# Two graph layers on one core: table joins spread, fetched rows joined later, small weights prepared ahead

## What is computed

```python
h = maximum(layernorm(x), 0)
x = x + max over neighbours j of h[j, :]          # layer 0
h = maximum(layernorm(x), 0)
hw = h @ W;  a1, a2 = a[:128, 0], a[128:, 0]
e = (hw @ a1)[:, None] + (hw @ a2)[None, :]
e = where(e > 0, e, 0.2 * e); e = where(adj > 0, e, -9e15)
x = x + elu(softmax(e, axis=1) @ hw)              # layer 1
```

## Time and profile before the change

| | |
|---|---|
| runs | 738.23, 739.4, 741.63 us; median 739.4 |
| profiled execution | 738.5 us, its span (first to last instruction) 736.6 us |
| PE busy | 643.8 us, 87% |
| DVE busy | 564.0 us, 77% |
| POOL busy / ACT busy | 366.4 us, 50% / 306.1 us, 42% |
| mean granted clock of PE | 0.956 |
| moved by DMA | 173.32 MB, 235 GB/s on average |
| take of pair 0 / of pair 127 / first weights of layer 1 start at | 25.85 / 438.87 / 448.88 us |

### The profile page before, as it was taken

The page is one execution under the profiler, slowest core; times in us unless marked ns, Lnnn a source line. Parts: engine busy times, 40 slices in busy tenths (PEclk is TensorE's granted clock), DMA queues, the critical chain, the costliest instruction groups (busy, mean ns, idle before and its releaser), DMA issues.

```text
span 736.6 us, 15876 instructions
## 1 busy us (share of the span) xinstructions
PE 643.8 (87%) x6200; PEld 525.3 (71%) x6200; DVE 564.0 (77%) x1296; ACT 306.1 (42%) x554; POOL 366.4 (50%) x357
## 2 busy tenths in 40 slices
PE   1849999899999999799899567989689999999994
PEld 0536667667777677576577356889588999999994
DVE  9829666767868786677768379789578999889893
ACT  1735556567667665466457325514033111001000
POOL 0512147657677765777767776645200474214030
PEclk9988999999999999999999868999989999999998
DMA  9999999999999997999889941428332445444400
GB/s 298 315 392 339 408 339 338 337 345 336 326 349 342 326 319 230 240 362 385 264 248 204 303 151 40 154 84 203 108 115 63 177 151 183 164 138 151 149 16 17
DMA packets 66925, 173.32 MB, mean 235 GB/s; under 512 B 7984, under 2 KB 12720, under 8 KB 62624
## 3 DMA queue, kind: packets, MB, share of 16 engines
q1 hardware_dynamic: 53776, 138.75, 53.9%
q0 software_dynamic: 13072, 33.51, 16.7%
HBM read 125.37 MB, written 46.86 MB: 234 GB/s over the span
## 4 chain that ended last, share of the span: by engine, by line
PE 52%; DVE 15%; DMA 14%; POOL 11%; issue 7%; ACT 1%; DVEq 0%; SPq 0%; POOLq 0%; ACTq 0%
PE pick_ps L756 20%; PE pick_ps L638 10%; POOL found L409 7%; DMA found<-subset_max,rows_at 5%; PE late_ps L651 5%; PE late_ps L652 5%; PE late_ps L614 5%; PE order_ps L623 5%; DVE weight L1174 4%; DMA edge_units<-edge_t 4%; DVE acc L908 3%; DMA subset_max<-keys 2%; PE late_ps L647 1%; DMA limit<-subset_max,spill_rows 1%; POOL h_lo L349 1%
## 5 line engine op out<-in xcount | busy, mean ns | idle before, releaser
L409 POOL DMA_INDIRECT found<-subset_max,rows_at x256 | 256.6, 1002 | 143.0 <-issue 58.9
L756 PE MATMUL pick_ps<-keys,weight 128*128 128x129 f32 x1792 | 214.5, 281 | 18.3 <-DVE weight L1174 18.3
L756 PEld LDWEIGHTS pick_ps<-keys,weight 128*128 128x128 f32 x1792 | 209.6, 197 | 23.8 <-DVE weight L1174 21.9
L1174 DVE SCALAR_TENSOR_TENSOR weight<-limit,curves_sb,stage 128x512 f32<-128x512 f32 x256 | 199.8, 821 | 14.5 <-PE pick_ps L756 2.0
L908 DVE TENSOR_TENSOR acc<-pick_ps,acc 128x1024 f32<-128x1024 f32 x120 | 146.5, 1221 | 69.3 <-PE pick_ps L638 68.5
L447 ACT ACTIVATE first<-order_ps 128x1024 f16<-128x1024 f32 x128 | 131.0, 1023 | 122.8 <-PE order_ps L623 120.7
L652 PE MATMUL late_ps<-bit_n,first 128*128 128x128 f16 x1024 | 131.5, 222 | 0.0
L651 PE MATMUL late_ps<-bit_w,edge_t 128*128 128x128 f16 x1024 | 131.4, 222 | 0.0
L638 PE MATMUL pick_ps<-first,h_hi 128*128 128x512 f16 x256 | 99.7, 390 | 18.5 <-DVE acc L908 18.4
L614 PEld LDWEIGHTS late_ps<-ident_h,stage 128*128 128x128 f16 x1024 | 69.5, 100 | 60.8 <-ACT edge_t L440 14.6
L652 PEld LDWEIGHTS late_ps<-bit_n,first 128*128 128x128 f16 x1024 | 101.8, 99 | 8.2 <-issue 0.6
(11 more groups left out here) (197 smaller groups left out, 570.2 us busy)
## 6 DMA issues: line engine op xcount, KB each, us to landing
stage<-adj SPq DMA_DIRECT2D x64, 1024.0 KB, 9.4
edge_units<-edge_t SPq DMA_DIRECT2D x64, 512.0 KB
stage<-edge_units SPq DMA_DIRECT2D x32, 1024.0 KB, 4.9
subset_max<-keys POOLq DMA_DIRECT2D x13, 512.0 KB, 8.3
found<-subset_max,rows_at POOLq DMA_INDIRECT x256, 6.7
best<-x SPq DMA_DIRECT2D x4, 512.0 KB, 6.3
subset_max<-x POOLq DMA_DIRECT2D x4, 512.0 KB, 10.6
spill_max<-keys POOLq DMA_DIRECT2D x4, 512.0 KB, 14.0
```

Of the source, the lines that this page charges most:

```text
L409: nc.gpsimd.indirect_dma_start(found[:, n % NG, s, :], None, subset_max, bass.IndirectOffsetOnAxis(rows_at[:, n, s:s + 1], 0)).then_inc(ga ...
L756: last = nc.tensor.matmul(out_ps(q, b), weight[:, n % WEIGHTS, b * P:(b + 1) * P], wh[:, c, :], start=c == 0 and starts(q, b), stop=c == C ...
L1174: V.scalar_tensor_tensor(out=weight[:, n % WEIGHTS, :], in0=limit[:, q % 4, :], scalar=slope[:, c:c + 1], in1=units[:, m % EDGES, k * TI:( ...
```

## The change

- **Tables.** The joins 0 to 3 stay behind takes 0 to 3; the others follow two takes apart, behind takes 6, 8, ... 18 (`CHAIN_AT`). The four clears leave the end of the table stores and stand ahead of the fetches of blocks 4, 6, 8 and 10.
- **Ring.** `KEPT` is 4. The room comes from `weight`, which now lies in `first`; the lists' buffers move to the second half of `keys` (`spare_room`). One small constant is dropped (`tri_h`, for which `order_w` with another offset serves), another is f16 (`places`).
- **Joins of fetched rows.** The first two blocks of a tile are joined at pairs 15, 0 and 1 instead of 13 to 15 (11 to 13 in the last tile), the other two at pairs 8 to 10 instead of 5 to 7 of the next tile. Blocks 24, 25 are joined behind the loop; those at mixes 5, 40, 46, 56 move to 18, 42, 60, 67; the one at 33 stays.
- **Lists.** Fetched ahead of blocks 18, 26 and 30 (before: 16, 24, 31), stored ahead of 20, 28, 31, loaded ahead of 21, 28, 31. Joined at take 101, mix 2 and mix 52 (before: takes 88, 121, mix 50). Merged at take 112 and mixes 20, 58 and 68, the last list in halves (before: take 102, ahead of layer 1, mix 58).
- **Small weights.** `W` and `a` are loaded ahead of x; POOL widens `a` before its first work on `h_lo`; PE transposes `W` ahead of the first `flip` and multiplies behind it; ACT's three copies stand ahead of its first root and behind its third `select`.

```diff
-        KEPT = 3
+        KEPT = 4
-        weight = sb("weight", [P, 6, TI], F32)
+        CHAIN_AT = (0, 1, 2, 3, 6, 8, 10, 12, 14, 16, 18)
+        spare_room = keys[:, 1, :, :].rearrange("p r w -> p (r w)")
+        weight = first.rearrange("p s w -> p (s w)").bitcast(F32).rearrange("p (s t) -> p s t", t=TI)
...
+                sp.dma_start(w_sb[:, 0:D], w).then_inc(w_in, 16)
+                sp.dma_start(a12[:, 0:1], a[0:D, :]).then_inc(w_in, 16)
+                sp.dma_start(a12[:, 1:2], a[D:2 * D, :]).then_inc(w_in, 16)
                 for i in range(4):
                     sp.dma_start(xs[:, i * QUARTER:(i + 1) * QUARTER, :], x_rows[:, i * QUARTER:(i + 1) * QUARTER, :]).then_inc(x_in[i], 16)
                 for n in range(STAGES):
                     load(n)
-                sp.dma_start(w_sb[:, 0:D], w).then_inc(w_in, 16)
-                sp.dma_start(a12[:, 0:1], a[0:D, :]).then_inc(w_in, 16)
-                sp.dma_start(a12[:, 1:2], a[D:2 * D, :]).then_inc(w_in, 16)
...
+                    if n in (4, 6, 8, 10):
+                        i = n // 2 - 2
+                        nc.gpsimd.dma_start(spill_dram[:, i * QUARTER:(i + 1) * QUARTER, :], spare(3)).then_inc(spill_clear, 16)
+                    if n in (18, 26, 30):
+                        spill_fetch((18, 26, 30).index(n))
+                    if n in (20, 28):
+                        spill_store((20, 28).index(n))
+                    if n in (21, 28):
+                        spill_load((21, 28).index(n))
+                    if n == 31:
+                        spill_store(2)
+                        spill_load(2)
...
-                    if g < len(CHAINS):
-                        chain(g)
+                    if g in CHAIN_AT:
+                        chain(CHAIN_AT.index(g))
...
-                    if q >= 1 and p >= 13 and q < LAST:
-                        halve(ROWS * (q - 1), 2, p - 13)
-                    if q >= 2 and 5 <= p < 8:
-                        halve(ROWS * (q - 2) + 2, 2, p - 5)
-                    if q == LAST and 11 <= p < 14:
-                        halve(ROWS * (q - 1), 2, p - 11)
+                    if 2 * STEPS - 1 <= g < PAIRS - 1 and (g + 1) % STEPS < 3:
+                        halve(ROWS * ((g + 1) // STEPS - 2), 2, (g + 1) % STEPS)
+                    if g >= 2 * STEPS + 8 and 8 <= p < 11:
+                        halve(ROWS * (q - 2) + 2, 2, p - 8)
```

117 lines of the change are left out of this document (53 added, 64 removed).

## The result

The changed kernel took 710.7 us (median of 4 runs, 705.3 to 712.3), the kernel before 738.8 in the same comparison: a ratio of 0.960, with a 95% interval of 0.954 to 0.966. The forecast was 709.5, the range 700 to 724. The profiled execution took 712.3 us (span 710.5), against 738.5 (span 736.6).

What follows compares the result with a forecast made beforehand. PE sets the pace at 2.78 us a pair, so only longer steps can be won. Terms -6 - 9.5 + 1 + 2 - 9 - 12.3 + 4.6 = -29.2 us from 738.5 gave 709.5 us, range 700 to 724.

Steps and rivals of the forecast that it cites:

- Table joins: Opening, behind take 4: the fifth join, moved behind take 6, waits 8.8 us instead of 14.33; -6 us (bounds -2, -9).
- Edge ring: Takes 19 and 36 to 40: a fourth slot and spread clears remove both late-store waits; -9.5 us (bounds -5, -9.7).
- Price of the spread: After take 18: POOL's fetches start about 6 us late, join at take 31 just in time; +1 us (0 to +6).
- Start: Before take 0: loads of W and a ahead of x delay everything by 1.0 to 5 us; +2 us.
- Joining later: Takes 88 to 110: first list and blocks 18, 19 joined later, so waits for fetched rows go; -9 us (-6, -10.5).
- End of layer 0: Takes 121 to 125: blocks 24, 25 fetched before the second list, joined behind the loop; -12.3 us (-9, -13.3).
- Layer 1: From first weight to end: moved joins and merges cost time; five parts together +4.6 us (bounds -1 and +11).
- (a): Mix 17: joins of blocks 26, 27 and merge of list 1 where DVE has no weights stored; +2.6 us.
- (b): Third list, from known to merged: 37.3 us unchanged; DVE still waits some 9 us, in one place.
- (c) to (e): Later joins +1.5, block 31 just in time for mix 67 +1, half the merge at mix 58 gone -0.5.
- Bound by bytes: Opening, 25.8 to 93 us: DMA limited near 365 GB/s, less won, POOL's start later; 719 us, chance 0.17.
- Layer 1 at its upper bound: Blocks 30 and 31 queue behind list 3, joins stall: +11 instead of +4.6, 716 us; chance 0.15.

## Why the prediction was right, point by point

- **Bound of the kernel.** Right: PE's pace of 2.78 us a pair is unchanged (takes 24 to 28 need 10.97 us in every kernel here), and the gain came from the longer steps alone.
- **Table joins, -6.** Measured -5.8; a wait of 8.2 us where 8.8 was said, because the store took 15.1 us and not 15.9. Undoing the spread gave 4.6 of it back in these takes, and 2 to 4 us net.
- **Edge ring, -9.5.** Measured -4.4 and -6.5, together -10.9, beyond the bound of -9.7, and half of the cause was wrong. The wait at take 19 went because the clears no longer stood in one burst: it is gone without the fourth slot, and in the kernel before with the clears alone moved. The prediction names slot and clears and books both waits to the ring as one term; that the first came out at -4.4 says nothing for the ring. The second is the slot's with 4.1 of 6.5 us. In return the ring is needed near take 100 as well (3.7 us), which the prediction doesn't have.
- **Price of the spread, +1.** Measured +1.0 for takes 19 to 36. POOL's first fetch came at 101.1 us, near the 100 that was said, but 15.2 us behind take 18 and not 12.5. So the join behind take 31, forecast as just in time, waited 3.6 us; 2.2 were caught up by take 36. The number is right partly by luck, as the wait was not in it.
- **Start, +2.** Measured +1.5, by the loads of x. The copies on ACT cost nothing, as said; with x first they did, because `a` then landed later, the exception that the prediction had made.
- **Joining later, -9.** Measured -9.0; the old places of the list cost 6.3 us of waiting and 6 us in all.
- **End of layer 0, -12.3.** Measured -12.6. The place of the join carries 8 to 9 us of it; the order of the fetches, which the prediction also named, hardly matters. The rest, with the early attention vector, was not undone by itself.
- **Layer 1, +4.6: the term that was mis-sized.** Measured +8.4 from one execution to the other. Its parts: (a) mixes 0 to 28, forecast +2.6, measured 47.9 - 43.5 = +4.4; (b) came out, from the list known (461.3) to its merge (498.67) 37.4 us, and a wait of 8.5 where 9 was said; (c) to (e), forecast +2, measured +2.7 by mix 72; and 1.6 more by mix 100 (0.3 of all this is gone by the end). Behind mix 72 no edit of the change stands. The windows of mixes 72 to 100, before and after, hold the same 200 matmuls at another clock:

```profile
553.10:576.90 23.80, 23.01 (x200) 22.53 (x201) 19.94 (x30) 5.82 (x14) 0.00 (x0) 1.00 0.36 126
```

```profile
525.70:551.10 25.40, 24.60 (x200) 24.13 (x201) 20.30 (x30) 5.82 (x14) 0.00 (x0) 0.93 0.33 119
```

The variant with x first, whose layer 1 is the changed one, took 23.85 us for these mixes, as before the change; the other six took 25.5, and the old layer 1, with the clears moved, 26.6. So the 1.6 us need not be the change's. From mix 100 to the last weight all fourteen traces took 143.4 us. The windows for mixes 17 to 28, before and after, show what (a) had left to its upper bound:

```profile
476.30:492.40 16.10, 13.45 (x112) 12.79 (x112) 14.34 (x44) 1.05 (x2) 6.79 (x7) 1.00 0.28 91
```

```profile
442.60:462.20 19.60, 15.09 (x112) 14.71 (x112) 17.64 (x47) 0.94 (x2) 11.21 (x10) 0.83 0.25 88
```

The same 112 matmuls kept PE busy 1.6 us longer, at a clock of 0.83 instead of 1.00, behind a gap of 3.46 us; the rest of the 3.5 us is idle time. This part is the change's: all nine kernels with that gap took 19.6 to 20.3 us for these mixes at 0.83, and the two with the old layer 1 took 16.0 and 17.1. The window over the whole layer, to be set beside that of the kernel before, shown with the clears:

```profile
414.40:710.50 296.10, 263.76 (x2184) 256.45 (x2184) 244.36 (x462) 55.37 (x141) 111.01 (x87) 0.94 0.37 122
```

PE was busy 263.8 us instead of 258.5 for the same work, so 5.3 of the 8.4 us are time in which PE ran, and 3.1 are waits; the prediction's sum counted waits alone. A second reason is the base: the kernel before with its clears moved has the same layer 1 and took 293.6 us for it, and the seven variants of the changed kernel whose layer 1 is untouched took from 293.7 to 296.8. Up to mix 72, where all edits stand, the eight traces of the changed layer 1 took 110.3 to 111.7 us and the two of the old one 104.2 and 107.4. There the change costs 3 to 7.5 us, and the forecast's 4.6 lies inside. The forecast took one profiled execution's 287.7 for the kernel's, and these runs don't fix the cost closer.
- **Rivals.** Bound by bytes: out, by 383 GB/s in the same stretch. Layer 1 at its upper bound: 8.4 of 11 in the trace, the nearest to coming true. DMA-bound and slower: out. Waits just move: out for both middle terms (takes 88 to 110 and 121 to 125 are 9.0 and 14.0 us shorter). Better than forecast: its start (+1) was near, its even layer 1 was not seen.

## What to carry to other kernels

Before a wait is booked to the buffer that ends it, ask what made the transfer late: here a burst of clears stood in front of one store, and moving them did what a fourth buffer was credited with at that place. Where an engine waits for a result that takes a known time, count the steps that could be done in that time and put the wait behind them: the first table join that waits behind take 9 rather than 6, a join and a merge ahead of a wait rather than behind it, and a root looked up four weights later won, with the third list's earlier store, another 13 to 17 us. And a stretch of one profiled execution is a sample: the part with the most clock changes should be read in two executions before a term is set against it, and part by part: here nearly all of the difference between executions lay ahead of mix 100.
